# Three parts of a fused graph-network kernel rearranged: its start, its end, and how the row maxima travel through DRAM

## The reference, cut to what matters

```python
def L0(h, a, kernel, attention_kernel, attention_kernel_2, bias):   # 4 heads of 16
    feats = einsum('bnf,hfo->bhno', h, kernel)
    scores = einsum('hbnd,hbdm->hbnm', h @ attention_kernel, h @ attention_kernel_2)
    masked = a * scores
    masked = where(masked >= 0, masked, 0.2 * masked) / 4 + where(a == 0, -1e9, 0)
    attn = softmax(masked, axis=-1) * (a != 0)
    return relu(attn @ feats + bias)                                  # heads side by side
def L1(x, a):  return ((a + eye) @ x) / sum(a + eye, axis=2)
def L2(x, a):  return a @ (x @ weight) + bias
def L3(x, a):  t = a @ x;  return where(t > 0.5, 1, 0)
x = norm(x + L0(x, adj)); x = norm(x + L1(x, adj)); x = norm(x + L2(x, adj)); x = norm(x + L3(x, adj))
```

## Time and profile before

| | us |
|---|---|
| median of 3 runs (lowest, highest) | 1761.11 (1760.62, 1762.89) |
| the profiled execution | 1762.62 |
| its span, first to last instruction | 1760.8 |
| busy: PE, DVE, ACT, POOL | 1454.2, 1384.5, 1241.6, 1089.5 |
| mean granted TensorE clock, share of full | 0.912 |

### The profile page before, as it was taken

How to read it: one execution, slowest core, us unless ns; L and a number is a source line. 1 busy time by engine, 2 the same in 40 slices (tenths; PEclk the granted TensorE clock), 3 DMA queues, 4 the chain that set the end, 5 groups by cost and what they waited for, 6 DMA issues and landing times.

```text
span 1760.8 us, 22052 instructions
## 1 busy us (share of the span) xinstructions
PE 1454.2 (83%) x7728; PEld 718.8 (41%) x7728; DVE 1384.5 (79%) x1623; ACT 1241.6 (71%) x1475; POOL 1089.5 (62%) x581
## 2 busy tenths in 40 slices
PE   4487889898889889888889888988899987888745
PEld 3233334444444444444444443444444443344313
DVE  3567788878898778888888778987888788888654
ACT  2377878777687777777787777777687777777521
POOL 1056676676676666676576667776666766766642
PEclk9788989999899999999999999999999999999767
DMA  5413142122413133221522234130432214000000
GB/s 77 61 32 48 31 66 40 46 30 39 70 31 46 26 52 51 52 36 26 68 40 43 25 55 58 39 44 17 63 46 52 30 37 55 21 12 24 15 6 9
DMA packets 55067, 71.42 MB, mean 41 GB/s; under 512 B 21814, under 2 KB 42814, under 8 KB 54958
## 3 DMA queue, kind: packets, MB, share of 16 engines
q0 software_dynamic: 13824, 18.01, 13.7%
q1 hardware_dynamic: 41134, 52.01, 11.4%
HBM read 102.29 MB, written 3.26 MB: 60 GB/s over the span
## 4 chain that ended last, share of the span: by engine, by line
PE 45%; DVE 24%; issue 12%; ACT 11%; SPq 3%; POOL 3%; DMA 2%; ACTq 0%; POOLq 0%; DVEq 0%
PE M L586 11%; DVE RUN L823 9%; PE M L535 9%; PE Z L496 8%; PE Z L498 7%; ACT LS L677 6%; PE Z L509 4%; DVE LS L837 4%; ACT LS L685 3%; SPq L286 2%; DVE X L922 2%; POOL LS L403 2%; PE Z L596 2%; DVE RUN L820 2%; PE Z L657 2%
## 5 line engine op out<-in xcount | busy, mean ns | idle before, releaser
L403 POOL TENSOR_TENSOR LS<-LS,MB 125x1000 f32<-125x1000 f32 x384 | 894.7, 2346 | 489.4 <-DVE LS L837 334.8
L823 DVE TENSOR_TENSOR RUN<-Z,RUN 125x1000 f32<-125x1000 f32 x528 | 631.0, 1195 | 208.7 <-ACT LS L677 203.4
L677 ACT ACTIVATE LS<-Z 125x1000 f32<-125x1000 f32 x576 | 574.5, 998 | 262.0 <-PE Z L498 261.4
L685 ACT ACTIVATE LS<-LS 125x1000 f32<-125x1000 f32 x576 | 594.5, 1033 | 71.3 <-POOL LS L403 56.2
L496 PE MATMUL Z<-AT,BI 126*125 126x500 fp8e4 x1152 | 386.0, 418 | 140.1 <-DVE RUN L823 107.0
L535 PE MATMUL M<-LS,V 125*18 125x500 f32 x2304 | 326.7, 642 | 57.8 <-ACT LS L685 57.0
L498 PE MATMUL Z<-FS,FO 96*125 96x500 bf16 x1152 | 360.1, 395 | 0.0
L837 DVE TENSOR_TENSOR LS<-LS,MB 125x1000 f32<-125x1000 f32 x192 | 283.2, 1475 | 4.9 <-DMA MB<-row_maxima 2.8
L496 PEld LDWEIGHTS Z<-AT,BI 126*125 126x125 bf16 x1152 | 140.7, 146 | 282.9 <-DVE RUN L823 164.5
L498 PEld LDWEIGHTS Z<-FS,FO 96*125 96x125 bf16 x1152 | 165.5, 144 | 111.4 <-issue 21.3
L586 PE MATMUL M<-AT,XP 125*128 125x500 fp8e4 x756 | 206.8, 396 | 0.7 <-ACTq L735 0.7
(11 more groups left out here) (118 smaller groups left out, 1039.6 us busy)
## 6 DMA issues: line engine op xcount, KB each, us to landing
MB<-row_maxima SPq DMA_DIRECT2D x48, 488.3 KB
A<-in_adj_dram POOLq DMA_DIRECT2D x96, 183.1 KB, 4.8
FO<-PARTS SPq DMA_DIRECT2D x192, 46.9 KB, 2.1
FS<-PARTS SPq DMA_DIRECT2D x192, 46.9 KB, 2.1
XP<-in_x_dram SPq DMA_DIRECT2D x8, 375.0 KB
XA<-in_x_dram SPq DMA_DIRECT2D x8, 375.0 KB
out_dram<-X SPq DMA_DIRECT2D x7, 375.0 KB
row_maxima<-LMAX SPq DMA_DIRECT2D x48, 3.9 KB
```

What stands on the lines that cost most here:

```text
L403: nc.gpsimd.tensor_tensor(rows, rows, MB[:, u % 2, :, :], ALU.subtract).then_inc(sub_pool, 1)
L677: nc.scalar.activation(LS[:P, q % RL, :, :], banks("Z", q)[:P], ACT.Prelu, alpha=0.2).then_inc(bent, 1)
L685: nc.scalar.activation(rows, rows, ACT.Exp, scale=0.25).then_inc(exps, 1)
L823: nc.vector.tensor_tensor(run, z, run, ALU.max).then_inc(maxed, 1)
```

## The change

- **Maxima.** The write of LMAX is two DMAs, of 112 and of 13 partitions; MB has 128 partitions and the read back repeats over 128. load_rows is likewise two DMAs.
- **Start.** WA and WV are issued by ACT ahead of its first copy. SP issues W2, the biases and XA before it waits for the low parts. FS of the first pair is issued by ACT behind its low-part wait, FO by SP. Six of DVE's seven memsets of AT go to POOL, interleaved with the loads of tiles 3 to 6, and count among the constants that all engines wait for (CONSTS 22). PE makes FE between the turns of the tiles. DVE waits for weights_in in the first keep.
- **End.** The last unit's maxima are turned at step 576, not 577. From step 558 of the subtractions on all are DVE's. At q = 594 DVE runs neighbours and the norm of two chunks, at 596 scales them; in the end loop normalise is cut into centred and summed, with scaled of the chunk before between them, and each low part comes one chunk earlier.

```diff
-CONSTS = 16
+DRAIN = QN - LAG
+CONSTS = 16 + RS - 1
+LAST_ROWS = QN + 18
...
-        MB = sb("MB", [P, 2, 2, C], f32)
+        MB = sb("MB", [128, 2, 2, C], f32)
...
+        def turned_at(q):
+            return NU - 1 if q == QN else unit_at(q, RT_AT) if q < QN else None
...
+        def by_vector(e):
+            return e % TURN == TURN - 1 or e >= DRAIN
+        def by_dve(e):
+            return min(e, DRAIN) // TURN + max(e - DRAIN, 0)
         def by_pool(e):
-            return e // TURN * (TURN - 1) + min(e % TURN, TURN - 1)
+            return e - by_dve(e)
...
             def load_rows(b, dst, sem_):
-                sp.dma_start(dst.rearrange("p (s k) f -> p s k f", k=ST), x_v[b]).then_inc(sem_, 16)
+                for rows in (slice(0, 112), slice(112, P)):
+                    sp.dma_start(dst[rows].rearrange("p (s k) f -> p s k f", k=ST), x_v[b][rows]).then_inc(sem_, 16)
...
-                sp.dma_start(spread[u % 2].rearrange("(h i c) -> i h c", i=P, c=ST),
-                             LMAX[:, u % 2, :].rearrange("p (h c) -> p h c", c=ST)).then_inc(max_out[u % 2], 16)
-                sp.wait_ge(max_out[u % 2], 16 * (u // 2 + 1))
+                for rows in (slice(0, 112), slice(112, P)):
+                    sp.dma_start(spread[u % 2].rearrange("(h i c) -> i h c", i=P, c=ST)[rows],
+                                 LMAX[rows, u % 2, :].rearrange("p (h c) -> p h c", c=ST)).then_inc(max_out[u % 2], 16)
+                sp.wait_ge(max_out[u % 2], 32 * (u // 2 + 1))
...
                 sp.dma_start(MB[:, u % 2, :, :].rearrange("p h c -> p (h c)"),
-                             spread[u % 2].partition_broadcast(P)).then_inc(mb_in[u % 2], 16)
+                             spread[u % 2].partition_broadcast(128)).then_inc(mb_in[u % 2], 16)
...
             load_rows(0, XF, xf_in)
-            sp.dma_start(WA[:, 0, :, :], wself.rearrange("h f o -> f h o")).then_inc(early_in, 16)
-            sp.dma_start(WA[:, 1, :, :], wother.rearrange("h f o -> f h o")).then_inc(early_in, 16)
-            sp.dma_start(WV[:, :, :], wv.rearrange("h f o -> f h o")).then_inc(early_in, 16)
-            load_features(0, 0)
-            load_features(0, 1)
             sp.dma_start(WW[0:F, 1, :], w2).then_inc(weights_in, 16)
...
             load_rows(0, XA[:, :, :], xa_in)
+            sp.wait_ge(lo_ready, NS)
+            for h in range(2):
+                load_parts(FO[:, h, :], fo_in[0], 1, h)
+            load_features(0, 1)
...
+            for n in range(1, RS):
+                const(nc.gpsimd.memset(AT[96:P + 1, n, :, :, :].rearrange("p q n k -> p (q n k)").bitcast(f32), ONES8))
+                if n <= ST:
+                    load(RA + n - 1)
...
-                if 0 <= e < QN and e % TURN != TURN - 1:
+                if 0 <= e < QN and not by_vector(e):
                     subtract(e)
...
-            for c in range(NS):
-                features("FE", c, Z[:, c, 0], pre_xts[c]).then_inc(pre_fe, 1)
             for k in range(ST):
                 if k:
                     pe.wait_ge(at_ready, k)
                 turn_adj(k, M1)
+                if k < NS:
+                    features("FE", k, Z[:, k, 0], pre_xts[k]).then_inc(pre_fe, 1)
...
+            act.dma_start(WA[:, 0, :, :], wself.rearrange("h f o -> f h o")).then_inc(early_in, 16)
...
+            act.wait_ge(lo_ready, NS)
+            for h in range(2):
+                for n, pair in enumerate(TERMS):
+                    act.dma_start(FS[n * D:(n + 1) * D, h, :], PARTS[h * D:(h + 1) * D, pair[0], :]).then_inc(fs_in[0], 16)
...
-            for n in range(RS):
+            for n in range(1):
                 nc.vector.memset(AT[96:P + 1, n, :, :, :].rearrange("p q n k -> p (q n k)").bitcast(f32), ONES8)
...
+                if u == 0:
+                    dve.wait_ge(weights_in, 4 * 16)
...
-            dve.wait_ge(weights_in, 4 * 16)
+            dve.wait_ge(const_ok, CONSTS)
...
+                if q == LAST_ROWS:
+                    for n in range(3):
+                        neighbours(B - 1, n)
+                    for c in range(NS - 1):
+                        normalise(0, c)
+                if q == LAST_ROWS + 2:
+                    for c in range(NS - 1):
+                        scaled(0, c)
+            normalise(0, NS - 1)
+            low_part(0, 0)
+            low_part(0, 1)
+            scaled(0, NS - 1)
+            low_part(0, NS - 1)
+            for l in range(1, 4):
+                add(l - 1, 0)
+                normalise(l, 0)
+                for c in range(1, NS):
+                    add(l - 1, c)
+                    centred(l, c)
+                    scaled(l, c - 1)
+                    summed(l, c)
+                    if l < 3:
+                        low_part(l, c - 1)
                 scaled(l, NS - 1)
                 if l < 3:
-                    for c in range(1, NS):
-                        low_part(l, c)
+                    low_part(l, NS - 1)
```

More of the change, by code:

```diff
@@ L253, in adj_resnorm @@
                 ring.append(("W", *w_at(q)))
-            if unit_at(q, RT_AT) is not None:
-                ring.append(("RT", unit_at(q, RT_AT)))
+            if turned_at(q) is not None:
+                ring.append(("RT", turned_at(q)))
             if slice_at(q):
@@ L637, in _ @@
                     turn_back(*w_at(q))
-                if unit_at(q, RT_AT) is not None:
-                    turn_run(unit_at(q, RT_AT))
+                if turned_at(q) is not None:
+                    turn_run(turned_at(q))
                 if slice_at(q):
@@ L783, in _ @@
                     expo(q - EXP_AT)
-                if unit_at(q, MAX_AT) is not None:
-                    bend_maxima(unit_at(q, MAX_AT))
+                if turned_at(q - 1) is not None:
+                    bend_maxima(turned_at(q - 1))
             def end_highs(l, c):
@@ L1024, in normalise, with summed @@
                 follow(c)
+            def summed(l, c):
+                rows = slice(ST * c, ST * (c + 1))
+                y, squares = Y[:, rows, :], SQ[:, rows, :]
                 step(c, nc.vector.tensor_tensor(squares, y, y, ALU.mult))
@@ L1044, in low_part @@
                                         ALU.subtract).then_inc(end_low, 1)
-            for l in range(4):
-                for c in range(NS):
-                    if l:
-                        add(l - 1, c)
-                    normalise(l, c)
-                    if c:
-                        scaled(l, c - 1)
-                    if c > 1 and l < 3:
-                        low_part(l, c - 2)
+            for c in range(NS):
+                rest(0, c, Z[:, c, 1], SPARE[:, c % 2, :])
+                low(0, c, SPARE[:, c % 2, :])
@@ new lines, in _ @@
+            for k in range(ST):
+                keep_adj(0, k, M1)
+            dve.wait_ge(const_ok, CONSTS)
+            for q in range(END):
+                b, r = graph_at(q)
+                if q < QN:
+                    maximum(q)
+                if slice_at(q):
+                    g, k = slice_at(q)
+                    keep_adj(g, k, banks("T", g, k)[:, 0, :])
+                if unit_at(q, G_AT) is not None:
+                    keep(unit_at(q, G_AT))
+                if w_at(q):
+                    add_up(*w_at(q))
+                if turned_at(q) is not None:
+                    row_maxima(turned_at(q))
+                if feature_at(q) and feature_at(q)[0] == "FT":
+                    _, bb, c = feature_at(q)
+                    rest(bb, c, M1, REST[:, :])
+                    dve.wait_ge(rest_ready, NS * bb + c + 1)
+                    dve.sem_inc(m1_read, 1)
+                if r in NEIGHBOURS and 1 <= b < B:
+                    neighbours(b - 1, NEIGHBOURS[r])
+                if layer_at(q, 0):
+                    mean(*layer_at(q, 0))
+                if layer_at(q, CENTRE):
+                    centre(*layer_at(q, CENTRE))
+                if layer_at(q, SUM):
+                    add_squares(*layer_at(q, SUM))
+                if layer_at(q, SCALE):
+                    scale(*layer_at(q, SCALE))
+                if r in MIDDLES and b + 1 < B:
+                    low(b + 1, MIDDLES[r], REST[:, :])
+                e = q - LAG
+                if 0 <= e < QN and by_vector(e):
+                    subtract(e)
+                if q == LAST_ROWS:
[6 more added lines that the diff above has]
+                        scaled(0, c)
```

83 lines of the change are left out of this document (22 added, 61 removed).

## The result

| | before | after |
|---|---|---|
| median of 4 runs each, one chip (lowest, highest), us | 1760.86 (1760.32, 1762.89) | 1684.8 (1683.04, 1685.42) |
| the profiled execution, us | 1762.62 | 1685.22 |
| its span, us | 1760.8 | 1683.4 |
| mean granted TensorE clock | 0.912 | 0.936 |

The ratio of the times is 0.9564, with a 95% interval of 0.9548 to 0.9581: 76 us less, where 66 were forecast. 1684.8 lies inside the range, near its lower end. The intervals of this document leave out two executions that came out far above the others of their kernel (2578 us once for the maxima alone, 1991 us once for the kernel before).

The account below looks back on a forecast made before the run. No engine was full (PE busy 83%); waits bound the kernel: a bias DMA, MB's broadcast and POOL's subtractions. Start -25, body -23 and end -19 made -67 us from 1762.6, 1695.6, put at 1695 us; range 1680 to 1716.

Parts of the forecast that it names:

- The start: Before the first maxima: earlier weights, DMAs issued on two queues and memsets on POOL save 25 us (20 to 31).
- The microsecond that WV was to gain: At the start: WV, issued by ACT, lands at 11.5 us, 1 us better than before.
- POOL's memsets: At the start: two memsets after the last tile load, 2.1 us each (1.3 to 3.5), open the loop at 32.5.
- rival B: At the start: issues go one after the other or memsets take 3.5; start -20, 1700 to 1701 us; chance 0.13.
- The body: Units of all graphs: MB landing earlier over sixteen DMA engines saves 23 us (15 to 26).
- capping them: Body: ACT's waits following MB landings, capped at 2.3 us each (first at 5): 12.7 in graph 0, 14 later.
- such a wait passes on whole: Body: from units 1 to 3, a 7.00 us ACT wait lengthened the interval 6.9 us; 0.9 passed on was used.
- The end: Drain and last layers: an earlier turn, subtractions by DVE alone and earlier low parts save 19 us (13 to 23).
- The step on MB: Drain: with the earlier turn and faster broadcast, the last MB lands at 1651.5, 4.4 us earlier.
- A: Body, graphs 1 to 7: PE or DVE takes over as the bound; body only -8, 1711 us; chance 0.17.
- C: Maxima's path: broadcast stays on five engines at 6.7 us, the second write costs; body +5, 1726 us; chance 0.08.
- D: Every unit: broadcast on sixteen engines waits for the busiest, drawing an adjacency tile; slower, 1790 us; chance 0.02.

Follow-up runs that it names:

- the maxima alone: The kernel before with only the maxima's write in 112 and 13 partitions and read back over 128: 1725.91 us, ratio 0.9802.
- the start alone: The kernel before with only the new start and the row loads in two parts: 1738.29 us, ratio 0.9877.
- both further edits: The changed kernel with the weights' loads first and the feature loads one step later, behind the spread of the maxima: 1665.69 us, ratio 0.9465.
- the features' edit: The changed kernel with each pair's 24 feature DMAs issued one step later, behind the spread of the maxima: 1671.54 us, ratio 0.9486.
- the end alone: The kernel before with only the change's end part: 1739.55 us, ratio 0.9898.

## Why the prediction was right, and where not

**The start: right in size (-24.9 against -25 in this trace, -22 to -24 in four others, 20 by the time of the start alone), with another last wait.** Low parts at 20.0 (20.2 said), the issues side by side, the bias's wait gone, first maximum at 36.19 (35.6). The microsecond that WV was to gain is not borne out: in four of the five traces WV came no earlier than with the old start. And the loop was not opened by POOL's memsets. One takes 1.37 us and not the 2.1 I took between two bounds; they end at 30.93. What opened it is FS: I gave it the landing of before, 2.1 us, and got 30. The last of the twelve is issued by 27.95 and lands at 33.08; the page's median for those from ACT is 4.9 us. Two errors of opposite sign met, and an early WV, and the number was good by luck. Of rival B the issues did not go one after the other and the memsets did not take 3.5; a gate stayed all the same, at a price near to nothing.

**The body: the mis-sized term, -23 said, about -35 measured.** That MB would land 2.6 us earlier over sixteen engines held: 6.7 to 3.8 us. Two steps after it were wrong, in opposite directions.

First, ACT's waits shrank less than I said: by capping them I had 12.7 us in graph 0 and 14 later, 26.7 together (times 0.9 that is 24, not the 23 that I wrote). Measured between first and last RMAX: 40.7 to 23.5, 17.2. What stayed in graph 0, 12.2 us in four waits, is mostly the spread behind the feature DMAs; moving those took it to 0.7.

Second, and more, a microsecond of such a wait was not worth 0.9 on the wall but, on the average, 1.5 to 2. This is the step "such a wait passes on whole", read from one pair of units. Across the runs:

| compared | ACT's wait for POOL, first to last RMAX | body | us per us |
|---|---|---|---|
| after against before | -17.2 | -36.8 | 2.1 |
| read over 128 against before | -20.9 | -34.5 | 1.7 |
| after against after with read over 125 | -12.9 | -25.3 | 2.0 |
| both further edits against after | -10.2 | -15.4 | 1.5 |

The price is not one number. The two long waits that the features' edit took away passed on nearly whole, as I had said (11.7 us of wait, 12.2 of time). Graph 0 as a whole gained 14.4 us for 8.1 us of wait, graphs 1 to 7 gained 22.4 for 9.0, where the forecast's products are 11.4 and 12.6. So the larger part of the miss is in the later graphs.

The pair that I chose misled. Its first unit (27.45 us, no ACT wait) has a floor of its own: it takes 27.0 to 27.5 us in every variant. The second, which waited 7.00 us, ran 34.38; I took 27.45 for its undisturbed length. With the spread ahead of the features it takes 26.5. Better is unit 3. Two rows of the kernel before (units 3 and 4, from RMAX to RMAX), then the same two with the read over 128 alone (columns: length, busy time of PE, PEld, DVE, ACT and POOL, clock, DMA share, GB/s):

```profile
179.17:207.93 28.76, 23.38 (x111) 10.57 (x110) 21.36 (x24) 22.97 (x26) 20.13 (x10) 0.88 0.16 25
207.93:235.28 27.35, 23.82 (x113) 10.84 (x112) 23.48 (x22) 22.85 (x26) 18.20 (x8) 0.88 0.19 47
```

```profile
172.77:197.34 24.57, 20.77 (x112) 9.22 (x111) 21.31 (x24) 22.62 (x26) 18.09 (x10) 1.00 0.21 30
197.34:222.12 24.78, 20.98 (x114) 9.30 (x113) 21.70 (x24) 22.51 (x26) 18.36 (x9) 1.00 0.19 46
```

In unit 3 ACT waited 2.6 us for POOL, and the unit was 4.2 us longer. In unit 4 it was 1.0 and 2.6. PE has the same number of matmuls within one and is busy 2.6 and 2.8 us longer, at a clock of 0.88 instead of 1.00. With the write split alone ACT waits 0.8 us in unit 3, and it is 2.8 us shorter than before, at a clock of 0.93. Where it falls can be seen in the kernel before, inside unit 3:

```profile
190.00:194.00 4.00, 3.92 (x20) 1.38 (x19) 3.38 (x3) 2.23 (x3) 2.82 (x2) 1.00 0.05 21
194.00:198.00 4.00, 0.20 (x5) 0.09 (x8) 1.77 (x2) 3.19 (x5) 4.00 (x2) 1.00 0.00 0
199.00:205.00 6.00, 6.00 (x24) 3.39 (x24) 5.28 (x9) 5.14 (x6) 4.33 (x2) 0.50 0.00 1
206.00:210.00 4.00, 4.00 (x21) 2.82 (x24) 1.80 (x3) 1.25 (x3) 1.51 (x1) 1.00 0.00 0
```

And where PE's pause comes from, in its timeline:

```profile
191.18 10.08 POOL L403 TENSOR_TENSOR LS<-LS,MB 125x1000 f32<-125x1000 f32 x4 [3.54 <-DMA MB<-row_maxima]
...
193.54 1.04 ACT L685 ACTIVATE LS<-LS 125x1000 f32<-125x1000 f32 x1 [1.76 <-POOL LS L403]
...
197.94 1.03 PE L535 MATMUL M<-LS,V 125*18 125x500 f32 x8 [3.80 <-ACT LS L685]
```

MB is late, PE stands nearly idle from 194 to 198, and then runs at 0.50 of its clock, the lower level of 1.2 GHz, for six microseconds, fully busy: 24 matmuls where the four microseconds behind them hold 21. With the read over 128 the clock is 1.00 through both units. The wait is paid once while it lasts and again when work resumes.

In graphs 1 to 7 the clock moved little (0.94 before, 0.95 after), though on so long a stretch this is not nothing: PE is busy 1192.0 us there instead of 1203.8, with as many matmuls within 11. DVE is busy 1132.8 us instead of 1149.3. They are 22.4 us shorter for 9.0 us less of ACT's wait (22.2 for 11.5 with the read over 128 alone). There a late MB can have another price, which the waits of ACT don't hold. One unit of graph 1 in the kernel before:

```profile
449.15 5.27 POOL L403 TENSOR_TENSOR LS<-LS,MB 125x1000 f32<-125x1000 f32 x2 [7.39 <-DMA MB<-row_maxima]
...
449.64 2.63 DVE L909 SCALAR_TENSOR_TENSOR Y<-MEAN,Y 125x768 f32<-125x768 f32 x1
...
452.19 3.29 DVE L837 TENSOR_TENSOR LS<-LS,MB 125x1000 f32<-125x1000 f32 x1
...
456.64 1.09 PE L496 MATMUL Z<-AT,BI 126*125 126x500 fp8e4 x2 [5.79 <-DVE RUN L823]
```

POOL, held for 7.39 us, subtracts without a pause, and DVE's operations beside it stretch: the centring takes 2.63 us where the changed kernel has 0.95 at this step, the subtraction 3.29 instead of 1.19, and PE waits 5.79 us for the maximum that is queued behind them. Over the whole trace DVE's subtraction takes 1475 ns on average before, 1479 with the write alone and 1455 with the read over 125; it is 1416 and 1402 with the reads over 128 and 126 alone, 1375 after (these last 1375 and the 1455 hold twelve subtractions more in the drain, where POOL does not run). The second price is shown in the one unit and fits the means; that it makes up the 22.4 us is not shown. Against it speaks the features' edit, which took 35 us off POOL's waits for MB in these graphs and left them 2.1 us shorter: with ACT's wait unchanged, POOL's waits of up to 4.4 us cost next to nothing there; those of the kernel before went up to 7.4. How the 22.4 us divide between the clock, the stretched operations and the spread of single graphs (up to 5 us) stays open.

**The end: right in kind, -17 measured against -19.** DVE's subtractions alone: held, and worth 2.7 us in the end of the run that undid them (5.8 by medians whose intervals overlap). Layers 1 and 2: -3.3 and -2.7 where -3.1 and -2.6 were said; PE's first layer starts 2.5 us after the last keep (2.4 said). The step on MB was right but empty: it lands before DVE asks for it (its wait is 0.89 us with the end alone and none here). What ran ahead of it was DVE's queue, which stood 3.51 us at 1595.93 for a product of PE (L617); counted with the earlier turn, PE starts its first layer 12 to 13 us earlier and not 14. Unforeseen was that PE's runs grew: from the start of the first layer's to its first sums 11.4 us instead of 10.3, in the second 11.1 instead of 10.55, at a granted clock of 0.77 and 0.80 instead of 0.86 and 0.84.

**The rivals.** A fell: PE did not take over, its share went from 83 to 85% only. C fell with the DMA share: more than five engines draw, and the two parts of the write cost nothing that can be seen. The Trainium skill's advice on disjoint partitions ("DMA: Bandwidth & Descriptors", section "Rules for kernel authors", "Don't bother — they serialize") was read by rival C as a cost of the split; no run shows one, since 1756.50 for the write alone (0.9957 to 1.0001) is neither a loss nor surely a gain. D fell: the longest wait for MB went from 9.8 to 8.0 us, and that one is the spread behind the features.

## What to carry to other kernels

The broadcast over 125 partitions used five DMA engines; giving the tile three rows more that nobody reads brought it from 6.7 to 3.8 us from issue to landing, and one row more gave the same time of the kernel. Price a wait by a unit's length with and without it in the same place of the schedule, over several units, and not by the wait: behind it came matmuls at half clock, and in one unit DVE operations stretched beside POOL's. And before a transfer is made faster, look at when it is issued: two moved lines were worth 13 us, nearly half of what the faster transfer was.

## What the runs showed of the hardware that I had not expected

- 126 partitions were as fast as 128 (1727.78 and 1729.11 us), 125 were not.
- The FS DMAs of SP's queue land 2.1 us after their issue (median), those that ACT issues beside SP's 4.9 (0.63 us per issue on both queues); two queues halved the time of issue, but from the first issue to PE's start they took 13.0 us instead of 17.6.
- POOL's memset of 30x1500 takes 1.34 to 1.39 us, about what DVE's does (1.31).
- A 16 KB load took 9.0 to 10.9 us to land beside three adjacency tiles, other weights and XA; issued ahead of them it took 2.7.
- A DVE operation of 0.17 us took 2.27 beside POOL's subtractions.
